# Cells rounded to two records, moves beside the phase of cells, and dense stages with a release per product bank

## What is computed

```python
x = _layernorm(x + _L0_gnn_ref(x, ...))   # two graph convolutions with layer norms and silu
x = _layernorm(x + _L1_gnn_ref(x, ...))   # attention over the edges, 4 heads, softmax per dst node
x = _layernorm(x + _L2_gnn_ref(x, ...))   # q, k, v attention, 8 heads, softmax per src node, edge bias
x = _layernorm(x + _L3_gnn_ref(x, ...))   # messages summed per dst node
# L0: agg = segment_sum(h[src] * norm[:, None], dst); return agg + h * (dinv * dinv)[:, None] + b
# L1: out = segment_sum(h[src] * alpha[:, :, None], dst); return tanh(out + bias)
# L2: out = segment_sum(attn[:, :, None] * v[col], row) @ Wo.T + bo; return layernorm(x + out) * ln_g + ln_b
# L3: agg = segment_sum(concat(x[src], x[dst]) @ W_msg + b_msg, dst); return concat(x, agg) @ W_upd + b_upd
```

## Time and profile before

| what | us |
|---|---|
| median of three runs | 11368.49 |
| the profiled execution | 11376.09 |
| its span | 11374.3 |
| DVE busy | 8091.7 (71%) |
| PE busy | 7268.5 (64%) |
| POOL busy | 5681.4 (50%) |
| ACT busy | 2645.4 (23%) |

### The profile page before, as it was taken

One profiled execution on the slowest core, in us unless ns is written; L12 is line 12 of the kernel. 1 busy time (PEld: TensorE's weight loads), 2 busy tenths in 40 slices (PEclk: granted clock), 3 DMA queues, 4 the chain that ended last, 5 costly groups with the idle time before them and its releaser, 6 DMA issues. The chain is left out here.

```text
span 11374.3 us, 187806 instructions
## 1 busy us (share of the span) xinstructions
PE 7268.5 (64%) x40485; PEld 5528.7 (49%) x40486; DVE 8091.7 (71%) x22008; ACT 2645.4 (23%) x7536; POOL 5681.4 (50%) x5516
## 2 busy tenths in 40 slices
PE   6999981033333359797456662776467777777398
PEld 5777761032222235454456661666455555555354
DVE  8999993079999950202899997888678888887601
ACT  0111110000000000101345550222146555555100
POOL 2777777710000023170477777777257777777000
PEclk9999995555555569898555555877689999999699
DMA  1000000045555558585779996888633333335187
GB/s 41 2 2 2 2 2 2 8 134 159 159 159 159 159 195 309 190 315 188 215 248 299 298 296 196 260 255 248 129 95 108 107 107 107 107 107 98 21 303 250
DMA packets 1175177, 1718.16 MB, mean 151 GB/s; under 512 B 312964, under 2 KB 877024, under 8 KB 1137056
## 3 DMA queue, kind: packets, MB, share of 16 engines
q1 hardware_dynamic: 565184, 1048.17, 27.6%
q0 software_dynamic: 204496, 358.11, 12.8%
q10 hardware_dynamic: 405264, 309.21, 9.1%
HBM read 1290.72 MB, written 424.01 MB: 151 GB/s over the span
## 5 line engine op out<-in xcount | busy, mean ns | idle before, releaser
L1451 POOL DMA_INDIRECT big<-tab_h,idx x1728 | 1985.2, 1149 | 1025.4 <-issue 523.1
L2355 POOL DMA_INDIRECT big<-tab_kv,idx x1728 | 1655.0, 958 | 762.6 <-issue 504.8
L922 POOL DMA_INDIRECT by_src<-big,h x1568 | 1566.9, 999 | 495.3 <-issue 476.0
L1629 DVE SCALAR_TENSOR_TENSOR acc<-big,room,acc 128x1280 f32<-128x1280 f32 (+1 forms) x960 | 1380.3, 1520 | 57.7 <-DMA big<-cells 57.5
L1900 DVE COPY acc<-banks 128x448 f32<-128x448 f32 x18 | 11.2, 625 | 1569.3 <-PE banks L1869 1567.7
L1264 DVE SCALAR_TENSOR_TENSOR acc<-acc,h,banks 128x128 f32<-128x128 f32 x4094 | 1101.1, 342 | 0.2
L953 POOL DMA_DIRECT2D room<-by_src x9 | 5.2, 584 | 2189.2 <-POOLq L2649 2189.2
L1869 PE MATMUL banks<-big,h 128*128 128x448 f32 x2744 | 1035.5, 541 | 18.3 <-DMA big<-cells 18.3
L1752 PE MATMUL banks<-big 128*128 128x132 f32 x3456 | 682.6, 362 | 349.9 <-DVE acc L1777 347.1
L1590 PE MATMUL banks<-we2t,acc 128*128 128x8 f32 x3456 | 804.7, 362 | 0.0
L649 PE MATMUL banks<-room 50*128 50x100 f32 x3136 | 794.5, 432 | 0.0
(11 more groups left out here) (488 smaller groups left out, 13681.0 us busy)
## 6 DMA issues: line engine op xcount, KB each, us to landing
big<-cells SPq DMA_DIRECT2D x262, 1568.0 KB, 8.4
cells<-acc SPq DMA_DIRECT2D x2049, 64.0 KB, 1.6
cells<-acc ACTq DMA_DIRECT2D x2048, 64.0 KB
big<-cells ACTq DMA_DIRECT2D x196, 640.0 KB, 6.4
head_rows<-big SPq DMA_DIRECT2D x432, 264.0 KB, 4.6
big<-head_rows SPq DMA_DIRECT2D x216, 528.0 KB
room<-w_rows SPq DMA_DIRECT2D x216, 512.0 KB
big<-loc_rows SPq DMA_DIRECT2D x216, 256.0 KB
```

The costliest lines, as they stand in the source:

```text
L922: pool.indirect_dma_start(k.by_src_dram, bass.IndirectOffsetOnAxis(k.pos[:, t:t + 1], axis=0), k.src_rec[:, t, :], None).then_inc(self.sca ...
L1451: pool.indirect_dma_start(k.stage[:, m % BODY, :], None, k.tab_h_dram, bass.IndirectOffsetOnAxis(k.idx[:, m:m + 1], axis=0)).then_inc(k.ga ...
L1629: ins = dve.scalar_tensor_tensor(mine, strip, k.small_asrc[:, src, h:h + 1], mine, ALU.min, ALU.max)
L2355: pool.indirect_dma_start(far[:, m % (G * RING), 0:2 * C], None, k.tab_kv_dram, bass.IndirectOffsetOnAxis(k.idx[:, m:m + 1], axis=0)).then ...
```

## The change

There are three parts. First, `UNIT` is 2, so a cell is rounded up to two records: T falls from 1728 to 1696 (`MOVES` = T / `UNIT` rises from 432 to 848, of 32 bytes for each record pair instead of 64 for four). Second, all moves leave the two gather phases and go behind the row gathers of POOL in `cells_phase`, in 53 chunks of 16, with a wait before every fourth that lets POOL run no further than four moves for each half turn of DVE's loop. Third, in the dense stages each product bank has its own count in `product` and `used`; the copies out of the banks (`turn`) come before the late jobs of the chunk before; the transposed rows have two rooms; rows that are the new `x` are scaled by ACT (`apply`, seven activations with scale and bias taken from `st`) instead of by DVE, and are transposed straight from `x` without a copy; gat_out stores k and v with one transfer from two rooms of its own; in msg_mid the transposes of the next chunk come ahead of the matmuls of this one (`eager`).

```diff
-UNIT = 4
+UNIT = 2
...
-CHUNK = 48
+CHUNK = 16
...
+    k.moved = [xx[:, Q // 2 + m * CHUNK * UNIT * 4:Q // 2 + (m + 1) * CHUNK * UNIT * 4]
+               .rearrange("p (j f) -> p j f", f=UNIT * 4) for m in range(4)]
+    k.move_to = [hh[:, m * CHUNK:(m + 1) * CHUNK].bitcast(I32) for m in range(4)]
...
@@ Moves.gpsimd @@
-    def gpsimd(self, pool):
+    def gpsimd(self, pool, pace):
...
                 t = c * CHUNK + j
+                pace(pool, t)
...
@@ cells_phase @@
+    moves = Moves(k, 0, CHUNKS)
...
             cell_rows(pool)
+
+            def pace(pool, t):
+                if t % 4 == 0:
+                    pool.wait_ge(made, t // 4 + 1)
+            moves.gpsimd(pool, pace)
...
@@ gather_phase @@
-        if chunks:
-            moves = Moves(k, *chunks)
-
-            @block.gpsimd
-            def _(pool):
-                moves.gpsimd(pool)
...
@@ Chunk @@
+    def norm_ahead(self, dve, i, n, per, src):
+
+        st = self.k.st
+        self.moments(dve, i, n, per, src)
+        dve.scalar_tensor_tensor(st[:, :, 11], st[:, :, 6], -1.0, st[:, :, 10], ALU.mult, ALU.mult)\
+            .then_inc(self.scaled, 1)
+
+    def apply(self, act, i, src, dst):
+
+        st = self.k.st
+        act.wait_ge(self.scaled, i + 1)
+        for b in range(BC):
+            last = act.activation(dst[:, b, :], src[:, b, :], ACT.Identity, bias=st[:, b, 11:12], scale=st[:, b, 10:11])
+        last.then_inc(self.applied, 1)
...
@@ dense_phase @@
-                dve.wait_ge(c.product, i + 1)
+                dve.wait_ge(c.product, i * width + 1)
                 after(c, dve, i)
-                if stores:
-                    dve.wait_ge(c.to_store, i + 1)
-                dve.sem_inc(c.used, 1)
...
+            for i in range(NCH + 1):
+                if i < NCH:
+                    work(i, early)
+                    turn(i)
+                if i:
+                    work(i - 1, late)
...
+            transposes(0)
+            for i in range(NCH):
+                if eager and i + 1 < NCH:
+                    transposes(i + 1)
+                c.select(i)
                 pe.wait_ge(c.copied, i + 1)
-                if i:
-                    pe.wait_ge(c.used, i)
                 for m, mat in enumerate(mats):
+                    if i:
+                        pe.wait_ge(c.used, (i - 1) * width + m + 1)
...
-                last.then_inc(c.product, 1)
+                    last.then_inc(c.product, 1)
+                if not eager and i + 1 < NCH:
+                    transposes(i + 1)
...
@@ stage_gcn_out @@
-        link(dve, dve.tensor_tensor(c.s, c.s, x, ALU.add))
-        link(dve, dve.tensor_tensor(c.s, c.s, x, ALU.add))
-        c.norm(dve, i, 2, 2, c.s, x)
-        copy(dve, c.y, x).then_inc(c.rows_ready, 1)
+        if i:
+            dve.wait_ge(c.applied, i)
+        link(dve, dve.scalar_tensor_tensor(c.s, x, 2.0, c.s, ALU.mult, ALU.add))
+        c.norm_ahead(dve, i, 2, 2, c.s)
...
@@ stage_gat_out @@
-        dve.wait_ge(c.room, i + 1)
-        link(dve, dve.tensor_tensor(c.o, product(k, 1), c.bc(k.v["L2_gnn_bk"][:, :]), ALU.add))
-        dve.tensor_tensor(c.s, product(k, 2), c.bc(k.v["L2_gnn_bv"][:, :]), ALU.add).then_inc(c.to_store, 1)
+        c.taken(dve)
+        if i >= 2:
+            dve.wait_ge(c.stored, (i - 1) * 16)
+        dve.wait_ge(c.product, i * 3 + 2)
+        link(dve, dve.tensor_tensor(room[:, :, 0:C], product(k, 1), c.bc(k.v["L2_gnn_bk"][:, :]), ALU.add))
+        c.taken(dve)
...
@@ stage_message_mid @@
-        copy(dve, c.y, by_blocks(k.x, i)).then_inc(c.rows_ready, 1)
+        dve.sem_inc(c.rows_ready, 1)
...
@@ message_out_phase @@
-                c.norm(dve, i, 1, 1, c.s, by_blocks(k.x, i))
-                dve.sem_inc(c.to_store, 1)
+                if i:
+                    dve.wait_ge(c.applied, i)
+                c.norm_ahead(dve, i, 1, 1, c.s)
...
@@ build @@
-        run(gather_phase, "gcn1", k.h, k.strips, k.total, (0, CHUNKS // 2))
+        run(gather_phase, "gcn1", k.h, k.strips, k.total)
...
-        run(dense_phase, "att_out", *stage_attention_out(k), [k.w["L2_gnn_Wo"]], ["turn", sqrt_job, sqrt_job])
+        run(dense_phase, "att_out", *stage_attention_out(k), [k.w["L2_gnn_Wo"]], (), [sqrt_job, sqrt_job, apply_job])
...
-            ["turn"])
+            rows=lambda k, i: by_blocks(k.x, i), eager=True)
```

## The result

The changed kernel took 11282.76 us (median of 5 runs, 11259.83 to 11297.88), the kernel before at its side 11372.8 us. The ratio is 0.9917, with a 95% interval of 0.9906 to 0.9929: faster by 0.8%, half of the forecast 1.7%, and above the top of the range.

| phase | before, us | after, us | difference | forecast |
|---|---|---|---|---|
| first work of the phase of cells begins at | 2269.5 | 2250.0 | -19.5 | 0 |
| phase of cells | 1800.8 | 1800.1 | -0.7 | 0 |
| gcn1 and gcn2 | 524.5, 524.9 | 524.7, 525.3 | +0.6 | 0 |
| gcn_out | 128.0 | 106.6 | -21.4 | -21 |
| maximum | 1554.3 | 1559.4 | +5.1 | 0 |

What follows compares the result with a forecast made beforehand. No engine bounds the whole span: DVE limits the loop of cells and dense stages, POOL attention. Moves 0, attention 40, weighted phase 33 and dense stages 117 sum to 190 us off 11376, giving 11186, range 11135 to 11245.

Steps and rivals of the forecast that it cites:

- Moves: Phase of cells: 848 moves fit beside DVE's loop and end 290 us before it, cost 0; leaving the gather phases gains nothing.
- Rival 1: Loop of cells: the moves' descriptors and small writes hold up DVE or stores, 34 to 85 us; chance 0.13.
- rival 3: Phase of cells: POOL's port is locked and POOL becomes the bound, slower than before at 12207 us; chance 0.03.
- Attention: Attention phase: 32 fewer columns take 40 us off POOL, which stays the limit.
- msg_mid: Dense stage msg_mid: PE and DVE run beside each other instead of taking turns, 87 becomes 55 us, a gain of 32.
- Rival 2: msg_mid and att_out: PE stays slow and the handovers give half, 25 us less gain, 11203 us; chance 0.11.
- gcn_out, gat_out and att_out: Three dense stages: less DVE work and fewer waits gain 21, 41 and 20 us.
- The output stage: Output stage: 11.8 us less DVE work, but ACT's scalings show and 1.3 x 7 come back, a gain of 3 us.
- The weighted phase: Weighted phase: four fewer batches gain 19 us and fewer slow padding columns 14, together 33, between 19 and 86.
- Rival 4: Weighted phase: the slow batches were chance and are absent, 53 us more gain, 11125 us; chance 0.05.

Runs made afterwards that it cites:

- the spread rows: Changed kernel with its attention loop moved by 41 met waits and the padding columns gathering 128 different table rows: 11146.72 us, ratio 0.9785.
- the kernel with 73 waits: Changed kernel with 73 more instructions on DVE, waits met at once, ahead of the attention loop: 11198.78 us, ratio to before 0.9841.
- that with 126 waits: Kernel before with 126 more met waits on DVE ahead of the attention loop: 11375.44 us, ratio 0.9999.

## Why the prediction was wrong

- **Moves: the number right, one reading of them wrong.** Forecast 0; the phase went from 1800.8 to 1800.1 us and PE's gather phases stayed. The moves' end was forecast 290 us before the loop's and came 294 before, since the pace of four in each half turn sets it. The prediction took the loop to be safe because its one-hot rows are not operations that hold POOL up. They are. Of the 848 moves 63 start while a one-hot row runs, and take 1.52 us in the mean; in the median they end 0.84 us after that row. The 785 others take 0.97. One of the 63, with the row beside it (start, duration):

```profile
3735.17 1.22 DVE L384 TENSOR_TENSOR room<-ramp_pair,room 128x2048 bf16<-128x2048 bf16 x1
3735.65 1.58 POOL L972 DMA_INDIRECT by_dst<-x,h  x1 [0.30 <-issue]
```

  This is the Trainium skill's rule (SBUF — State Buffer, section "SBUF: two separate sides"), by which whoever comes second waits for the whole instruction of the first; the section names for DVE, beside the two-port modes, operations with two inputs in SBUF, as these rows have, against a GpSimd operation that reads SBUF. The trace agrees in this direction only: 272 one-hot rows that start during a move take 1222 ns, like the 240 others. The price was small, 63 x 0.55 = 35 us of POOL's time inside its 294 us of slack. One-hot rows fill 625 of the loop's 1688 us, yet only 7% of the moves start in one: the wait for `made` lets POOL go when two of them have ended, so that its four moves run beside the sums. That the wait is what does this was not tested. Rival 1 is out, and so is rival 3: its lock is there, but not at 2.78 us for every move.
- **Attention: the step that failed.** "In attention that takes 32 x 1.264 = 40 us off POOL, which stays the limit." The term itself is right, as the kernels that keep the loop show (2202 to 2211 us with 1696 columns against 2250.5 with 1728 is 39 to 48 us; against the kernel before, whose gathers follow each other faster, 25 to 34 are left of it). What failed is that POOL stays the limit. The step took for granted that a phase whose code is not touched runs as before. The shorter dense stages moved DVE's loop so that it touches four blocks of 8 KiB, and it was fetched again in each of its turns, at 82 to 91 us. No rival had it.
- **msg_mid: failed.** "After, the two run beside each other." The order of PE was read rightly, but not what its transposes wait for: `rows_ready`, which DVE raises in `before` of the next chunk, behind `after` of the chunk before. PE's matmuls stand behind that wait. The stage fell by 13.2 us and not by 32. With the rows announced at once it is 34.2 us below the kernel before: the size was right for an overlap that the changed kernel does not have. Rival 2, half of the gain in msg_mid and att_out, was nearer for msg_mid, with the wrong cause (PE's granted clock went up there, from 0.72 to 0.79), and wrong for att_out, which gave all of its 20.
- **gcn_out, gat_out and att_out: 78.7 us of 82**, att_out up to the next phase. The sum is right, its terms only in part, and their errors cancel, which is luck. What ACT took over was worth 6.3, 5.5 and 8.4 us, not 9.4, 9.4 and 11.3; the rest, which no run took apart (the copy, the stores' rooms and the order of hand-overs), was worth 15, 31 and 12.
- **The output stage: wrong by its 3 us.** DVE is busy 25.2 us instead of 37.7 and the stage is no shorter: ACT's scaling shows whole, and with the scalings on DVE the stage is 1.4 us shorter.
- **The weighted phase: right in mechanism; 41.3 us and not 33 in this pair.** Over the kernels with 1696 columns and padding as it was, the phase takes 1089 to 1103 us, over the four of the kernel before 1129 to 1134, so the gain lies between 26 and 45 and 33 is not shown to be too low. That padding columns are slow because they gather one row was taken from the place where the slow stretch begins; the spread rows show it, with 43 to 51 us for 68 columns, 0.63 to 0.75 us each where 0.78 was forecast. Rival 4 is out.
- **19.5 us that nobody forecast** and whose cause is open. A scatter of the rank phase comes in the median 1.263 us after the last one in after and 1.274 before, 1568 times, though POOL's program up to there is the same in both. It is no chance and not the rounding: all eight kernels with the changed stages whose phase of cells I read, that of `UNIT` 4 too, begin it at 2250 to 2252 us, the four of the kernel before at 2267 to 2271.

The misses add up: 97 for attention, 19 for msg_mid, 4 for gat_out, 3 for the output stage, 5 for the maximum and 1 for the gathers, less 8 for the weighted phase, 1 for att_out and 20 for the early start, give about 100. The profiled execution of after, 11282.8, is 97 above the 11186 of the sum.

## What to carry to other kernels

- A long hardware loop that fits what an engine keeps of its program by size may still be fetched in every turn, by where it starts. After an edit look at the packets of the instruction queue in each phase, the untouched ones too, and at idle time that ends with "issue" once in a turn. A few waits that are met at once, put ahead of the loop, move it; the place that is right changes with every edit before it.
- To say that two engines overlap, follow each wait of the one back to the instruction that raises it on the other, and what that stands behind in its queue.
- Columns of padding that gather one and the same row are not cheap: give them different rows.
- A mean can hide a wait. 1013 ns a move looked like no contention, and was 785 moves of 0.97 us and 63 of 1.52; sort such operations by what the other engine runs when they start.

## What the hardware showed that I had not expected

- A loop of 323 instructions on DVE was kept when it touched three blocks of 8 KiB and fetched again when it touched four, though all of it is 20.7 KB; this fits all eight places tried, by a count of the built program. The Trainium skill's page (Runtime: NRT & Kernel Launch, section "Instruction fetch mechanics") has blocks of 16 KiB; the packets of DVE's loop are 8192 bytes, and places 129 and 195 of 256 decide against it. The fetches stalled DVE at one place for 3.4, 3.4 and 3.5 us a turn in the mean, and cost attention 0.5, 1.7 or 2.9 us a turn (29 / 53, 90 / 52, 153 / 53).
- In 150 us gathers of one row of 528 bytes by all lanes took 0.49 of all DMA engines' time, and the same amount from different rows 0.10. In attention no such end is to be seen: in the kernel with 73 waits POOL's gathers come 1.26 to 1.28 us apart up to the last 20 columns.
- A POOL transfer instruction takes 958 or 969 ns (medians, outside of one-hot rows) for the same scatter in two programs, over some 1400 of them. The longer time is that of the kernel before and of that with 126 waits, the shorter that of after and of three kernels with its stages.
- In the rank phase as in the loop of cells, a transfer instruction of POOL that starts during a 128x2048 one-hot row of DVE ends 0.84 us after it: 1.31 us where 0.47 us of the row were left, 1.53 where 0.70 were left.
